# Another order for the head of an attention and LoRA FFN kernel, with the first batch handled by pairs of tiles

## What is computed

```python
xn = layernorm(x)                                   # over the 256 features, eps 1e-5
q, k, v = xn @ wq.T + bq, xn @ wk.T + bk, xn @ wv.T + bv
attn = softmax(q @ k.T * 256 ** -0.5) @ v           # in each batch
W2 = W + up_aux @ (lora_up @ (lora_down @ down_aux))
out = x + attn + xn @ W2.T + b
```

## Time and profile before

| | |
|---|---|
| median of 3 runs | 516.13 us |
| the profiled execution | 516.27 us |
| its span in the trace | 514.5 us |
| busy: TensorE, VectorE, ScalarE, GpSimd | 503.9, 367.5, 276.6, 372.9 us |
| read from and written to HBM | 16.15 and 8.39 MB |

### The profile page before, as it was taken

The page is one execution under the profiler, slowest core; times in us unless marked ns, Lnnn a source line. Parts: engine busy times, 40 slices in busy tenths (PEclk is TensorE's granted clock), DMA queues, the critical chain, the costliest instruction groups (busy, mean ns, idle before and its releaser), DMA issues.

```text
span 514.5 us, 8100 instructions
## 1 busy us (share of the span) xinstructions
PE 503.9 (98%) x2948; PEld 446.3 (87%) x2948; DVE 367.5 (71%) x839; ACT 276.6 (54%) x589; POOL 372.9 (72%) x221
## 2 busy tenths in 40 slices
PE   4999999999999999999999999999999999999997
PEld 4777897989989898898989989898998989889897
DVE  4789876876679585895858767686757758476594
ACT  2755677265754747367382665736474462725450
POOL 2843795986879966999669978699688976671730
PEclk9999999999999999999999999999999999999999
DMA  8020005000050002200050100501003010000002
GB/s 241 38 83 0 1 4 203 1 41 2 1 204 1 41 1 85 121 2 41 1 189 17 43 2 0 205 1 42 0 22 103 1 42 1 41 1 2 41 1 82
DMA packets 8694, 25.04 MB, mean 49 GB/s; under 512 B 1850, under 2 KB 3792, under 8 KB 7760
## 3 DMA queue, kind: packets, MB, share of 16 engines
q1 hardware_dynamic: 7328, 24.38, 13.1%
q10 hardware_dynamic: 1328, 0.16, 0.2%
HBM read 16.15 MB, written 8.39 MB: 48 GB/s over the span
## 4 chain that ended last, share of the span: by engine, by line
PE 96%; DMA 1%; ACT 1%; DVE 1%; issue 0%; ACTq 0%; DVEq 0%
PE o_ps L1080 12%; PE o_ps L1079 11%; PE o_ps L1078 11%; PE g_ps L998 10%; PE g_ps L999 10%; PE g_ps L1000 10%; PE s_ps L998 9%; PE s_ps L999 8%; PE s_ps L1000 8%; DMA bk_col<-in_L_attn_bk 1%; PE o_ps L998 1%; PE g_ps L1020 1%; PE o_ps L1000 1%; PE o_ps L999 1%; ACT prod L607 1%
## 5 line engine op out<-in xcount | busy, mean ns | idle before, releaser
L507 POOL TENSOR_TENSOR p_lo<-s,p_hi 128x1024 fp32r<-128x1024 f32 x60 | 143.8, 2429 | 38.8 <-ACT p_hi L657 38.8
L650 ACT ACTIVATE s<-s,e 128x512 f32<-128x512 f32 x128 | 84.3, 714 | 116.2 <-DVE s L848 116.1
L1080 PE MATMUL o_ps<-v_lo,p_hi 128*128 128x256 f32 x480 | 136.1, 283 | 0.0
L1079 PE MATMUL o_ps<-v_hi,p_lo 128*128 128x258 f32 x480 | 135.1, 282 | 0.0
L1078 PE MATMUL o_ps<-v_hi,p_hi 128*128 128x258 f32 x480 | 134.6, 281 | 0.0
L1078 PEld LDWEIGHTS o_ps<-v_hi,p_hi 128*128 128x128 f32 x480 | 91.3, 190 | 1.7
L1079 PEld LDWEIGHTS o_ps<-v_hi,p_lo 128*128 128x128 f32 x480 | 91.1, 190 | 1.6
L1080 PEld LDWEIGHTS o_ps<-v_lo,p_hi 128*128 128x128 f32 x480 | 90.2, 188 | 0.0
L807 DVE SCALAR_TENSOR_TENSOR tile_max<-s_ps,e,tile_max 128x512 f32<-128x512 f32 x80 | 59.9, 749 | 32.7 <-PE s_ps L1000 30.6
L998 PE MATMUL s_ps<-xt_hi,zt_hi 128*128 128x512 f32 x192 | 74.9, 390 | 0.0
L999 PE MATMUL s_ps<-xt_lo,zt_hi 128*128 128x512 f32 x192 | 74.7, 389 | 0.0
(11 more groups left out here) (157 smaller groups left out, 989.2 us busy)
## 6 DMA issues: line engine op xcount, KB each, us to landing
out<-base SPq DMA_DIRECT2D x15, 512.0 KB, 2.7
x_sb<-in_L_attn_x SPq DMA_DIRECT2D x7, 1024.0 KB, 8.2
x_t<-in_x_t SPq DMA_DIRECT2D x6, 1024.0 KB, 6.0
x_sb<-in_L_attn_x SPq DMA_DIRECT2D x4, 256.0 KB, 6.5
out<-base SPq DMA_DIRECT2D x4, 128.0 KB, 1.9
s<-in_L_attn_wk SPq DMA_DIRECT2D x1, 256.0 KB, 3.0
s<-in_L_attn_wq SPq DMA_DIRECT2D x1, 256.0 KB, 5.7
s<-in_L_attn_wv SPq DMA_DIRECT2D x1, 256.0 KB, 7.1
```

The lines of the kernel that those rows point to most:

```text
L507: nc.gpsimd.tensor_tensor(p_pair(g, p_lo_sb, j), s_pair(j), p_pair(g, p_hi_sb, j).bitcast(f32), ALU.subtract).then_inc(p_lo_made, 1)
L650: nc.scalar.activation(s[:, n, :], s[:, n, :], ACT.Exp, bias=e[b % 2][:, n:n + 1]).then_inc(p_made, 1)
L1079: nc.tensor.matmul(o[:, 0:D + ONES], lo, v_hi[i][:, n, 0:D + ONES], start=False, stop=False)
L1080: mm = nc.tensor.matmul(o[:, 0:D], hi, v_lo[i][:, n, :], start=False, stop=last)
```

## The change

Host side: bq, bk and the two small LoRA factors come in one padded array (`small`, 128x58) in one transfer; before, ScalarE issued four transfers with single words and two more.

The head is rewritten. SyncE loads the first quarter of x ahead of wk, and V's weights ahead of the second half of x. TensorE starts with 24 products of the identity with itself, whose result nobody reads (`WARM`). A is made in plain fp32, not split. Batch 0 is handled by pairs of tiles j: `turn` (transposes), `first_v` (V alone, 256 columns), `first_z`, and `first_ffn` (FFN alone) behind the scores. ScalarE copies the FFN products into `base[1]` (`copy_first_ffn`), and GpSimd adds them to `base[0]` (`add_first_ffn`); VectorE added them before. `make_out` of batch 0 waits for that. GpSimd makes `prod` of batch 1 before the loop, and the first turns of its loop are written out.

The statistics of batch 2 move from the head to the end of VectorE's turn 0. With them ScalarE's `make_stat_cols(2)` moves by one turn, and VectorE's two `make_stat_row(2, ...)` move behind the shifts of turn 1.

```diff
@@ ScalarE's loop over g
-                if c == 0 and b + 2 < B:
+                if c == (0 if b else 1) and b + 2 < B:
                     make_stat_cols(b + 2)
@@ VectorE's loop over g
-                if b + 2 < B and c == 1:
+                if 0 < b < B - 2 and c == 1:
                     make_stat_row(b + 2, 0)
                 make_tile_max(g + 1, 0)
                 make_tile_max(g + 1, 1)
-                if b + 2 < B and c == 1:
+                if 0 < b < B - 2 and c == 1:
                     make_stat_row(b + 2, 1)
                 make_groups_lo(b, c, 0)
...
                 make_groups_lo(b, c, 1)
                 if g == 0:
                     make_out(b, c * QT + 1)
+                if g == 1:
+                    make_stat_row(2, 0)
+                    make_stat_row(2, 1)
...
                 make_groups_lo(b, c, 2)
+                if g == 0:
+                    nc.vector.tensor_reduce(e_row_sum[:, :], e_row, AXIS, ALU.add).then_inc(e_row_sum_made, 1)
+                    dve.wait_ge(x_loaded[0], DMA)
+                    make_stats(2, range(TILES))
+                    make_mean_var(2)
@@ ScalarE
+            def copy_first_ffn(j):
+                act.wait_ge(first_ffn_mm, j + 1)
+                nc.scalar.activation(base[1][:, 2 * j:2 * j + 2, :], pair(FIRST_FFN_BANKS[j][:, :]), ACT.Copy)\
+                  .then_inc(first_ffn_copied, 1)
...
+            for n in range(TILES):
+                make_second_xn(n)
+            act.wait_ge(bias_made, 1)
+            for j in range(PAIRS):
+                copy_first_ffn(j)
             make_p(0, 0)
-            make_group_hi(0, 2 * NT + 6)
             make_p(0, 1)
             make_p_hi(0, 0)
-            make_group_hi(0, 2 * NT + 7)
+            first_v_hi(3)
@@ GpSimd
+            def add_first_ffn(j):
+                pool.wait_ge(first_ffn_copied, j + 1)
+                tiles = slice(2 * j, 2 * j + 2)
+                nc.gpsimd.tensor_tensor(base[0][:, tiles, :], base[1][:, tiles, :], base[0][:, tiles, :], ALU.add)\
+                  .then_inc(first_ffn_added, 1)
@@ TensorE's head
+            pe.wait_ge(identity_made, 1)
+            for _ in range(WARM):
+                nc.tensor.transpose(s_ps[2][:, 0:PT], identity[:, :], identity[:, :])
...
+            for n in range(2, TILES):
                 scores(0, n)
...
-            for n in range(TILES):
-                group(0, 2 * NT + n)
+            for j in range(PAIRS):
+                first_ffn(j)
+            first_v(3)
```

More of the change, by code:

```diff
@@ L274, in two, with pair, group_bank, rstd_count @@
             return ap.rearrange("p (t n) -> p t n", t=DT)
[L276 to L283, removed]
-            return g_ps[k % 2]
[L286 to L296, removed]
+        def pair(ap):
+            return ap.rearrange("p (m n) -> p m n", m=2)
+        TURN_BANKS = (g_ps[0], g_ps[1], g_ps[1], s_ps[3])
+        FIRST_V_BANKS = (o_ps[0], g_ps[0], o_ps[0], o_ps[0])
+        FIRST_Z_BANKS = (s_ps[0], s_ps[1], o_ps[0], o_ps[1])
+        FIRST_FFN_BANKS = (o_ps[0], o_ps[1], o_ps[0], o_ps[1])
+        RANK_BANK = s_ps[3]
+        WARM = 24
+        def group_bank(k):
+            return g_ps[k % 2]
+        def rstd_count(b):
+            return len(STAGES) + b
+        def stage_of(tile):
+            return [first <= tile < end for first, end in STAGES].index(True)
+        def prods(b):
+            return PAIRS * (b + 1)
+        def pair_of_columns(j):
+            return slice(2 * j * PT, (2 * j + 2) * PT)
         LAST = CHUNKS * B - 1
@@ L332, in groups_at @@
                 return ()
[L333 removed]
+            return (FIRST_PLACES if b + 1 < EARLY else PLACES)[c].get(place, ())
         def groups_begun(g, n):
             b, c = divmod(g, CHUNKS)
[L339 removed]
+            count = groups(b, NG - 1) if b else 0
             for turn in range(c):
@@ L348, in _, with load_first @@
         def _(sp):
-            sp.dma_start(wk_sb, rows(wk)).then_inc(wk_loaded, DMA)
-            for j in range(4):
+            def load_first(j):
                 n = TILES // 4
@@ L567, in _ @@
         def _(act):
-            with nc.allow_non_contiguous_dma(reason="a few hundred words of biases and LoRA factors"):
-                act.dma_start(bq_col[:, :], column(bq)).then_inc(b_qk_loaded, DMA)
-                act.dma_start(bk_col[:, :], column(bk)).then_inc(b_qk_loaded, DMA)
-                act.dma_start(lora_down_t[:, :], lora_down.rearrange("r d -> d r")).then_inc(lora_loaded, DMA)
-                act.dma_start(lora_up_t[:, :], lora_up.rearrange("u r -> r u")).then_inc(lora_loaded, DMA)
@@ L1001, in split_products, with turn @@
                 return mm
+            def turn(j):
+                pe.wait_ge(xn_made, j + 1)
+                pe.wait_ge(first_xn_made, j + 1)
+                if j == 2:
+                    pe.wait_ge(turned_lo_made, 2)
+                elif j == 3:
+                    pe.wait_ge(mid_rank_made, 1)
+                for d in range(DT):
+                    for m in range(2):
+                        mm = nc.tensor.transpose(TURN_BANKS[j][:, (2 * d + m) * PT:(2 * d + m + 1) * PT],
+                                                 xn[:, 2 * j + m, d * PT:(d + 1) * PT], identity[:, :])
+                mm.then_inc(turned_mm, 1)
@@ new lines, in first_tokens, with first_v @@
+            def first_tokens(ps, j, right):
+                for m in range(2):
+                    t = slice((2 * j + m) * PT, (2 * j + m + 1) * PT)
+                    mm = split_products(ps[:, m * D:(m + 1) * D], lambda d: xt_hi[0][:, d, t], lambda d: xt_lo[0][:, d, t],
+                                        lambda d: vf_hi[:, d, right], lambda d: vf_lo[:, d, right])
+                return mm
+            def first_v(j):
+                pe.wait_ge(turned_lo_made, j + 1)
+                if j == 0:
+                    pe.wait_ge(wv_lo_made, 1)
+                elif j == 2:
+                    pe.wait_ge(first_v_lo_made, 1)
+                elif j == 3:
+                    pe.wait_ge(first_ffn_copied, 3)
+                first_tokens(FIRST_V_BANKS[j], j, slice(0, D)).then_inc(first_v_mm, 1)
```

510 lines of the change are left out of this document (291 added, 219 removed).

## The result

The changed kernel takes **523.48 us** (median of four runs, 521.90 to 524.68) against 516.07 us for the kernel before: a ratio of 1.0142, 95% interval 1.0115 to 1.0170. It is slower by 1.4%, as forecast (523.3 us, range 518.5 to 527). Its executions spread more than those of before: over all ten that were made in this study, four took 521.9 to 522.1 us, four 523.3 to 523.6 and two 524.7 to 524.8.

A forecast was written before the change was run, and what follows sets the result against it. TensorE, busy 503.9 of 514.5 us, was taken as the bound. Span 514.5 - 3.1 (head) + 1.1 (copies) - 0.5 (old wait) + 9.7 (rows) = 521.7, forecast time 523.3 us; range 518.5 to 527, its own bounds 520.5 to 525.5.

The forecast's parts named there:

- the statistics rows of batch 2: Turn 1: late VectorE transposes stall GpSimd's string, so TensorE's first P x V of turn 2 ends later; cost 9.7 us.
- The start and the pace: Head: useful work starts at 6.8 us and TensorE's pace doubles early; the batch loop starts 3.1 us sooner.
- the cost of the pace: Head: time lost to half pace after useful work starts; 0.5 us, bounds 0 and 5.2.
- that rule: Head: the full clock does not engage for transposes; pace cost near 5.2 us, sum 4.7 us higher.
- ScalarE after the head: Start of loop: TensorE's last scores wait for ScalarE's second raw copy; cost 1.1 us, bounds 0 and 1.5.
- M': Start of the batch loop in the changed kernel, the first scores of turn 1; forecast 45.1 us.
- the count of P: Times behind the loop start counted from P = M' + 1.1, the 1.1 us being the wait for the raw copy.
- The 4 us that should show at the last V groups: Batch 1's last V groups: about 4 us of the 9.7 us stall appears as TensorE waiting for their banks.
- the rival in which the pace falls back: New waits behind the head: TensorE drops to half pace, some 2.5 us remain, 526 us; chance 0.13.
- nobody waits for the late rows: Turns 1 and 2: GpSimd's delay falls to nothing and the head's gain remains, 513.6 us; chance 0.06.
- the pace does not double early: Head: loop start up to 4.7 us later, 528 us at the end, 526 midway; chance 0.15.
- gain and stall cancel: Head and turn 2: -4.2 - 0.5 + 8 = +3.3, 519.4 us; chance 0.05, and 0.02 for no change.

The follow-up runs named there:

- experiment 1: Kernel before, old head, with only batch 2's statistics columns moved to turn 1 and the transposes behind the V evictions: 525.74 us, ratio 1.0183.
- experiment 2: Changed kernel with batch 2's two statistics transposes earlier in turn 1: 514.74 us; with all handling of batch 2's statistics put back as before: 515.11 us.
- experiment 4: Changed kernel without its 24 identity products: 525.08 us; kernel before with those 24 products alone added: 516.12 us.
- the filler: Changed kernel with 24 identity products put into TensorE's 3.9 us wait ahead of the V groups of turn 1, place 3: 524.72 us.
- experiment 3: Changed kernel with batch 2's statistics handling put back as before, but VectorE's eight tiles of statistics cut in three pieces: 513.48 us, ratio 0.9956.

## Why the prediction was right

**Direction and place.** The largest term was the statistics rows of batch 2, and that is where the time went: experiment 1 makes the loss without the new head, and experiment 2 takes it away within the new head by moving two instructions.

**The start and the pace.** Useful work starts at 6.13 us (forecast 6.8), and the pace doubles within the identity products, so the cost of the pace is 0 instead of 0.5; what is left for gaps is 1.6 us instead of 1.0. The loop starts at 44.49 instead of 45.1 us. The half pace to 17.1 us that the prediction took for the head of before is that of one execution; in two others of the same head the pace had doubled by 14.3 us (experiment 4). The Trainium skill, TensorE: Matmul & The Clock Gate, Part 4, has it that the full clock does not engage for transposes. The trace disagrees: 24 transposes alone took 4.77 us (4.16 to 5.14 in seven other profiles) instead of 5.3, and the products right behind them ran at full pace; only in one execution of the changed kernel did they take 5.38, and there the pace doubled in the two products right behind. As the prediction priced that rule, the loop would have started at 49.8 us. The column of the profile that gives the granted clock reads 1.00 throughout the start, at half pace too; there only the duration of one product tells (2.05 us for the two products of 256 columns without the identity products, 1.03 behind them).

**ScalarE after the head.** The wait for the second raw copy exists; it is 0.3 us instead of 1.1 (the terms that the prediction lists come to 1.0).

**The statistics rows.** Forecast: transposes from M' + 55.8 to M' + 58.2; measured 99.31 to 101.67, M' + 54.8 to 57.2, with GpSimd idle from 90.0 to 101.8. From the end of the wait for the raw copy (44.79 in the count of P) to the end of the first P x V of turn 2 it is 86.3 us instead of 86.8, so the term is 9.2 instead of 9.7. The 4 us that should show at the last V groups are 3.9. The rest did not come as waits for p_lo alone: 2.6 us went into the half pace of those V groups, and 2.0 us are waits. The three come to 8.5 of the 9.2 us; no single row shows the rest.

**The sum.** These three sizes (0.6, 0.8 and 0.5) bring 521.7 us of span down to 519.8, which is the span of the short executions. The median lies 1.6 us above that one's time, and that is the rival in which the pace falls back: it was priced at 2.5 us, and the one longer execution that was profiled paid 1.4 to 1.6 of span for it; six of ten executions were longer by as much or more. So the median of 523.48 comes as close to 523.3 as it does by luck: terms 1.9 us too dear are made up by a fall of the clock that I had left to a rival (1.6) and by 0.3 us more between span and time. The narrower range of 520.5 to 525.5 does not come out of its own bounds, which give 520.0 at the low end and, with the late pace, 529.2 at the high one; the times lie inside either. The mechanism was right; the two sizes that I would now write otherwise are the rows, 9.2, and a fall of the clock behind the waits as part of the likeliest case. The Trainium skill, TensorE: Matmul & The Clock Gate, Part 1 (HAM oscillation), says that waits between strings of products bring the lower clock back; here the trace agrees, at 110 us behind 3.9 us of wait in every profile with the late rows and without the filler. At 131 us the clock fell in the one of four profiles of the changed kernel that had two waits of 1.4 us there.

**The rivals.** That nobody waits for the late rows fell: GpSimd's operations kept their durations (the four p_lo of turns 1 and 2 took 9.59 and 9.53 us, before 9.56 and 9.57). That the pace does not double early fell in every profile of the new head with its identity products. That gain and stall cancel fell.

## What to carry to other kernels

When the order of one engine is rewritten, look at what waits in the queues of the others for each instruction that is moved back: here two VectorE instructions of 1.2 us, put ten microseconds later in a turn of their own engine, cost some 9 us, because GpSimd's queue stands behind them and its slack is 3 us. A gain can need two edits together: neither the identity products alone nor the order alone gained more than the head's own scatter, both together 2.6 to 3.7 us. One profile of the kernel before is one execution: its head alone scattered by 1.1 us. After a gain at one place, look for the work that it uncovers there: the shorter head made a piece of 3.3 us of statistics that had been free cost 1.8, until it was cut in three.

## What the hardware showed that I had not expected

A fall of TensorE's clock costs only where TensorE is the later one. The same fall was free at 110 us, where GpSimd ended last, and cost 1.4 to 2.3 us at 131 us, where no other engine was behind. Products that merely keep the engine busy in a wait can therefore move the fall to a worse place, as the filler's profile shows.

Short waits can suffice for a fall. Where TensorE waited 1.3 to 1.4 us for p_lo twice or more, the clock fell: in the filler's profile, in the long execution of the changed kernel and in that of experiment 1. Where the first of two such waits was 0.4 to 0.8 us, it stayed up: in five profiles. Behind a single wait of 1.7 or 1.8 us, in the profiles of experiment 2, it stayed up too. In the head it fell in two profiles, behind a wait of 0.4 or 0.5 us for a load and one of 1.3 to 1.4 us; it stayed up in the seven others with the identity products, where one wait of 0.4 to 1.4 us and one of 0.2 stood. No run varies these waits by themselves, so this is what the profiles have in common and not a cause that was shown.

A change that leaves such waits behind makes the time spread: 521.9 to 524.8 us, where the version of experiment 3, without them behind the head, lies within 0.2 us.
